# A four-layer graph network on one core: half of layer 2's softmax division moved from VectorE to GpSimd

## What is computed

```python
attn = jnp.einsum('bhnd,bhmd->bhnm', q, k) * scale
attn = jnp.where(attn_mask[None, None] == 0, -jnp.inf, attn)
attn = jax.nn.softmax(attn, axis=-1)
o = jnp.einsum('bhnm,bhmd->bhnd', attn, v).transpose(0, 2, 1, 3).reshape(b, n, d)
...
x = _layernorm(x + _L2_gnn_ref(x, ...), axis=-1)
```

## Time and profile before

| what | value |
|---|---|
| median of 3 runs | 1381.44 us (1379.06 to 1381.63) |
| the profiled execution: its own time | 1379.5 us |
| its span, first to last instruction | 1377.7 us |
| TensorE busy | 1345.8 us (98%), 10460 matmuls |
| VectorE busy | 1113.5 us (81%) |
| ScalarE busy | 784.8 us (57%) |
| GpSimd busy | 135.1 us (10%) |
| mean granted TensorE clock | 0.994 |

### The profile page before, as it was taken

One profiled execution on the slowest core, in us unless ns is written; L12 is line 12 of the kernel. 1 busy time (PEld: TensorE's weight loads), 2 busy tenths in 40 slices (PEclk: granted clock), 3 DMA queues, 4 the chain that ended last, 5 costly groups with the idle time before them and its releaser, 6 DMA issues.

```text
span 1377.7 us, 27138 instructions
## 1 busy us (share of the span) xinstructions
PE 1345.8 (98%) x10460; PEld 1141.8 (83%) x10460; DVE 1113.5 (81%) x2441; ACT 784.8 (57%) x1444; POOL 135.1 (10%) x194
## 2 busy tenths in 40 slices
PE   8999999999999999999999999999999999999996
PEld 8888878888888888888888888888888888888785
DVE  6889878788888879788887888879888787869555
ACT  3455656556665665656556565665656456654544
POOL 4010111010010100001010000101001010101000
PEclk9999999999999999999999999999999999999998
DMA  5000010100000001010100000000000100100100
GB/s 178 9 17 24 1 25 31 24 30 15 8 30 23 30 15 38 0 23 30 23 30 15 23 15 23 30 23 31 12 11 30 23 32 1 39 9 1 46 0 31
DMA packets 54671, 34.54 MB, mean 25 GB/s; under 512 B 34912, under 2 KB 51552, under 8 KB 54624
## 3 DMA queue, kind: packets, MB, share of 16 engines
q1 hardware_dynamic: 52816, 29.43, 7.2%
q0 software_dynamic: 1248, 3.94, 0.9%
q10 hardware_dynamic: 560, 0.52, 0.1%
HBM read 12.92 MB, written 8.39 MB: 15 GB/s over the span
## 4 chain that ended last, share of the span: by engine, by line
PE 89%; DVE 7%; ACT 2%; issue 1%; DMA 0%; POOLq 0%; DVEq 0%; POOL 0%; ACTq 0%
PE banks L122 22%; PE banks L124 21%; PE banks L123 21%; PE banks L667 8%; PE banks L662 3%; PE banks L937 3%; PE banks L826 2%; PE banks L841 2%; PE banks L743 2%; PE banks L815 2%; ACT l_htok L1468 1%; PE banks L804 1%; PE banks L1036 1%; DVE l_r L2522 0%; PE banks L735 0%
## 5 line engine op out<-in xcount | busy, mean ns | idle before, releaser
L1604 ACT ACTIVATE l_r<-banks,bias_r 128x512 f32<-128x512 f32 x90 | 61.4, 682 | 177.4 <-PE banks L124 177.3
L264 POOL TENSOR_TENSOR l_rstd<-l_mv,eps 128x4 f32<-128x4 f32 x47 | 19.2, 409 | 908.6 <-DVE l_mv L258 908.6
L1468 ACT ACTIVATE l_rh_hi<-l_r 128x512 fp32r<-128x512 f32 x90 | 56.4, 627 | 62.1 <-DVE l_r L2511 61.9
L1621 ACT ACTIVATE banks<-banks,bias_h 128x512 f32<-128x512 f32 x96 | 63.4, 662 | 25.4 <-PE banks L124 25.0
L122 PE MATMUL banks<-l_rh_hi,u_hi 128*128 128x512 f32 x180 | 76.1, 423 | 0.1
L1615 ACT ACTIVATE banks<-banks,bias_z 128x512 f32<-128x512 f32 x96 | 63.5, 663 | 19.7 <-PE banks L124 19.7
L278 ACT ACTIVATE y<-l_sum,l_offset,l_rstd 128x256 f32<-128x256 f32 x124 | 69.1, 598 | 6.1 <-DVE l_offset L272 6.0
L124 PE MATMUL banks<-l_rh_lo,u_hi 128*128 128x512 f32 x180 | 71.1, 395 | 0.0
L123 PE MATMUL banks<-l_rh_hi,u_lo 128*128 128x512 f32 x180 | 70.7, 393 | 0.0
L667 PE MATMUL banks<-adj_t,y 128*128 128x128 f32 x544 | 68.1, 277 | 1.5 <-DVE l_otok L2460 1.5
L1537 ACT ACTIVATE l_qk<-banks 128x512 f32<-128x512 f32 x64 | 38.3, 598 | 54.1 <-PE banks L124 53.4
(11 more groups left out here) (308 smaller groups left out, 4418.2 us busy)
## 6 DMA issues: line engine op xcount, KB each, us to landing
x_tok<-in_x_dram SPq DMA_DIRECT2D x15, 512.0 KB, 3.5
l_res<-y SPq DMA_DIRECT2D x15, 512.0 KB, 2.9
out_dram<-l_res SPq DMA_DIRECT2D x15, 512.0 KB, 2.9
l_vpair<-l_vstage SPq DMA_DIRECT2D x32, 128.0 KB, 3.0
w_raw<-in_L_gnn_w_w_dram POOLq DMA_DIRECT2D x3, 512.0 KB, 7.5
qkv_raw<-in_L_gnn_w_qkv_dram POOLq DMA_DIRECT2D x1, 768.0 KB, 4.5
l_res<-in_x_dram SPq DMA_DIRECT2D x1, 512.0 KB, 5.4
u_raw<-in_L_gnn_u_w_dram POOLq DMA_DIRECT2D x2, 256.0 KB, 7.4
```

Source lines behind the costliest of these rows:

```text
L1468: return nc.scalar.activation(out, source, ACT.Copy)
L1604: nc.scalar.activation(own(u).r[:, m, :], rz(u)[:, m, :], ACT.Tanh, scale=0.5, bias=w.biases["r"][:, m:m + 1]).then_inc(s.r_ready.of(u), 1)
L1621: nc.scalar.activation(hv(u)[:, m, :], hv(u)[:, m, :], ACT.Tanh, bias=w.biases["h"][:, m:m + 1]).then_inc(s.hv_ready.of(u), 1)
```

## The change

The division of tiles 2 and 3 of each unit's `prob` goes to GpSimd as a new step `l2_divide(u)`, which waits once for `inv` and then issues both multiplications. VectorE keeps tiles 0 and 1 (`BY_VECTOR = 2`). TensorE's turns of tiles 2 and 3 wait on a new semaphore that GpSimd increments. The sums of the next unit wait for the semaphore of the unit before, since they overwrite `inv`. The step gets a place in GpSimd's list in the loop, in the fill and in the drain.

```diff
+BY_VECTOR = 2
...
+        self.l2_prob_divided = one("l2_prob_divided", TILES - BY_VECTOR)
...
+        @within
+        def l2_divide(u):
+
+            pool.wait_ge(*s.l2_inv.at(u, TILES + 2))
+            for t in range(BY_VECTOR, TILES):
+                nc.gpsimd.tensor_tensor(b.prob[:, t, :, :], b.prob[:, t, :, :],
+                                        b.inv[:, t, :].unsqueeze(2).to_broadcast([P, HEADS, NODES]),
+                                        ALU.mult).then_inc(s.l2_prob_divided.sem, 1)
+
         def body(i):
+            l2_divide(i + 1)
             l3_root(i - 1)
             l2_inner_root(i + 1)
             l2_outer_root(i + 1)
...
             l0_root(1)
             l1_root(1)
+            l2_divide(0)
             l2_inner_root(0)
             l2_outer_root(0)
             l0_root(2)
+            l2_divide(1)
             l2_inner_root(1)
...
             l3_root(11)
+            l2_divide(13)
             l2_inner_root(13)
             l2_outer_root(13)
             l1_root(14)
+            l2_divide(14)
             l3_root(12)
             l0_root(15)
             l2_inner_root(14)
             l2_outer_root(14)
             l1_root(15)
+            l2_divide(15)
             l3_root(13)
...
         def l2_turn_prob(u, t):
-            pe.wait_ge(*s.l2_prob_shared.at(u, t + 1))
+            if t < BY_VECTOR:
+                pe.wait_ge(*s.l2_prob_shared.at(u, t + 1))
+            else:
+                pe.wait_ge(*s.l2_prob_divided.at(u, t + 1 - BY_VECTOR))
...
         def l2_sum(u, t):
             dve.wait_ge(*s.l2_exp.at(u, t + 1))
+            if t == 0:
+                past(dve, s.l2_prob_divided, u - 1, TILES - BY_VECTOR)
...
             l2_normal(i + 1, 0)
             l2_normal(i + 1, 1)
-            l2_normal(i + 1, 2)
-            l2_normal(i + 1, 3)
             l3_reset(i, 0, 1)
```

More of the change, by code:

```diff
@@ L396, in __init__ @@
         self.l2_exp, self.l2_prob_turned, self.l2_prob_t = one("l2_exp", TILES), one("l2_prob_turned", TILES), one("l2_prob_t", TILES)
-        self.l2_pv_done, self.l2_inv, self.l2_prob_shared = one("l2_pv_done", TILES), one("l2_inv", TILES + 2), one("l2_prob_shared", TILES)
+        self.l2_pv_done, self.l2_inv, self.l2_prob_shared = one("l2_pv_done", TILES), one("l2_inv", TILES + 2), one("l2_prob_shared", BY_VECTOR)
+        self.l2_prob_divided = one("l2_prob_divided", TILES - BY_VECTOR)
         self.l2_o_hi, self.l2_o_lo = one("l2_o_hi", CH), one("l2_o_lo", CH)
@@ L2797, in fill @@
             l0_leaky(2)
-            l2_normal(0, 2)
             l0_masked(2)
@@ L2801, in fill @@
             l0_max(2)
-            l2_normal(0, 3)
             l0_shift(2)
@@ L2852, in fill @@
             l3_reset(0, 0, 0)
-            for n in range(2, 4):
-                l2_normal(1, n)
             l3_reset(0, 0, 1)
@@ L2967, in drain @@
             l3_reset(12, 0, 0)
-            for n in range(1, 4):
-                l2_normal(13, n)
+            l2_normal(13, 1)
             l3_reset(12, 0, 1)
@@ L3073, in drain @@
             l0_offset(15)
-            for n in range(4):
+            for n in range(2):
                 l2_normal(14, n)
@@ L3148, in drain @@
             l3_low_rh(13, 2, 1)
-            for n in range(1, 4):
-                l2_normal(15, n)
+            l2_normal(15, 1)
             l3_difference(13, 2, 0)
```

## The result

| | before | with the change |
|---|---|---|
| median | 1379.86 us (5 runs, 1379.06 to 1381.63) | 1402.8 us (5 runs, 1402.11 to 1404.43) |
| ratio | | 1.0163, 95% interval 1.0152 to 1.0174 |
| span of the profiled execution | 1377.7 us | 1400.8 us |

The account below looks back on a forecast made before the run. TensorE, 98% busy, bounds the kernel, so what counts is when its inputs come. Loop 10.0, units 1, 14, 13, 15, 0 4.3 + 4.8 + 1.4 + 1.4 + 0.6, clock 2.6: +25.1 on 1379.5, said 1405; range 1388 to 1416.

Parts of the forecast that it names:

- the clock: TensorE's clock at half after the idle gaps in units 1 and 14: 1.3 us each, 2.6 in all.
- The loop: Units 2 to 12: TensorE loads tile 3 at +3.45 us instead of +2.54, +0.91 per unit, 10.0 for 11.
- the price of a division on GpSimd: One 128 x 512 multiplication on GpSimd, unhindered: 1.2 us, between 1.05 and 1.48.
- my lower end: Price of a GpSimd division if its two reads take turns: 1.05 us, for a total of 1397.
- Hindrance: VectorE and GpSimd instructions with two SBUF inputs hold each other, one at a time, in order of asking.
- the one-sided rival: VectorE is never held, GpSimd waits for each of its instructions: +0.45 us per loop unit, +17, 1396; 15%.
- The rule of the Trainium skill: VectorE instruction with two SBUF inputs and GpSimd instruction reading SBUF share a read interface; the second "fully blocks".
- The relief: Two of four divisions leave VectorE, 1.2 us per unit, running into its 0.90 us idle before l3_offset: worth nothing.
- Unit 1: Fill: GpSimd's division stands behind layer 0's root, and tile 2 meets an l3_low_rh; tile 3 late, +4.3 us.
- Unit 14: Drain: VectorE's offset waits for layer 0's root behind GpSimd's two divisions and layer 3's root; +4.8 us.
- Units 13, 15, 0: 13 and 15: GpSimd's tiles come between VectorE's divisions, +1.4 us each; 0: GpSimd still at a root, +0.6.

Follow-up runs that it names:

- e4: Kernel before, plus unused GpSimd work in each loop pass: a 128 x 4 addition and a memset of 128 x 512; 1380.22 us, ratio 1.0001.
- e3: Kernel before, plus unused GpSimd work in each loop pass: a 128 x 4 addition and a two-input 128 x 512 multiplication; 1389.13 us, ratio 1.0069.
- e7: As e6, with unit 0's division ahead of layer 1's root for unit 1 in GpSimd's list; 1375.99 us, ratio 0.9965 to the kernel before.
- e1_order: Changed kernel with GpSimd's list mended: unit 1's division ahead of a root, two roots ahead of unit 14's division; 1394.35 us, ratio to before 1.0095.
- e2: Changed kernel with the list of e1_order, GpSimd dividing tile 3 alone and VectorE tiles 0, 1 and 2; 1390.15 us, ratio 1.0074.
- e5: Kernel before, plus unused GpSimd work in each loop pass: a 128 x 4 addition and a 128 x 512 copy; 1386.70 us, ratio 1.0046.
- e6: List of e1_order, but GpSimd divides tile 0 alone, beside VectorE's row sums, and VectorE tiles 1 to 3; 1377.77 us, ratio to before 0.9983.

## Why the prediction was right

1405 us were forecast, 1402.8 measured; the forecast's sum was +25.1 us, and the two spans differ by 23.1. The mechanism of the forecast is the one that the runs show; the terms of the loop and of unit 1 were mis-sized, and the clock's other stretches were missing. By shifts of TensorE's matmuls between the two traces:

- **The loop.** Forecast +0.91 us for each of 11 units, 10.0 in all; measured 0.62, 6.8 in all. The order of events is as drawn: division, GpSimd's tile, division, GpSimd's tile, and VectorE's second division ends 2.14 us after its first began (forecast 2.35), GpSimd's second tile 3.04 us after (forecast 3.41). The step that was off is **the price of a division on GpSimd**. I took 1.2 us, and it is 1.04 (unit 14: two in 2.04), my lower end. With 1.05 the forecast had 6.7 us for the loop. That the write adds nothing to the two reads fits this price, and in e4 a memset ran beside VectorE's divisions without holding them.
- **Hindrance.** Forecast as mutual and in order of asking; e3 shows VectorE held by 0.84 us for one multiplication of GpSimd. The time alone would not have told this from the one-sided rival: 0.62 us a unit lies between that rival's 0.45 and the forecast's 0.91. VectorE's divisions recorded with 2.14 us and e3 do. The rule of the Trainium skill that was weighed ("SBUF — State Buffer", section "Who interferes with whom") holds here from both sides, also in what it exempts: memsets of GpSimd and row sums of VectorE are not in the way (e4: divisions at 2.50 us; e7: sum at 0.68, GpSimd's division at 1.04).
- **The relief.** It was costed at nothing, with VectorE's wait for the root as its cover. Nothing was right, the cover was not needed: VectorE had no time freed. In unit 3 its divisions and the reset end 3.59 us after the first began (291.96 to 295.55), against 3.09 in the earlier trace rows, and it waits for the root for 0.90 us as before.
- **Unit 1.** Forecast +4.3 us and 1.3 for the clock; tile 3 came 3.4 us late, the slow clock behind it cost 1.6. The difference is again the price of a division, and that GpSimd's tile 2 did not meet the `l3_low_rh` that I let it meet: that one came only at 124.45, held up 4.05 us by ScalarE's copy.
- **Unit 14.** Forecast +4.8 and 1.3; measured 4.4 and 1.4. e1_order confirms both places: mended, unit 1 costs 1.3 us in place of 5.0, and unit 14 0.5 in place of 5.8, the slow clock included.
- **Units 13, 15, 0.** Forecast 1.4, 1.4, 0.6; measured 1.0, 1.7, 0.6.
- **Missing.** The clock stood at half for 6.8 us at the start in place of 3.4 (+1.5 us), and once at the entry of the loop (+2.2 us with the longer wait there); in the tail a slow stretch of the kernel before did not come (-1.6). The sum of all is 23.0 us, against 23.1 of the spans. That these three belong to the change is not shown. At the start e1_order has 77.7 us up to unit 0 like the changed kernel, e2 75.9, and no division of GpSimd's stands before that; at the entry of the loop other traces with nearly the same wait have no slow stretch; and in the tail e3 and e5 lack it too.

So the closeness of 1405 to 1402.8 is partly luck: 3.2 us too much in the loop and 0.9 in unit 1 stand against 2.1 us net that the clock did elsewhere.

## What to carry to other kernels

Moving elementwise work with two SBUF inputs from VectorE to GpSimd gave nothing here while VectorE itself ran such instructions: the two took turns, and GpSimd's turn was the longer one (0.84 us against VectorE's 0.60). Put GpSimd's piece beside VectorE instructions that read one SBUF input, even if that needs a small step drawn ahead. For a reduction e7 shows it. For a VectorE instruction with its other operand in PSUM only small additions show it: in the kernel before, GpSimd's 128 x 4 addition takes 0.20 us beside `late_lo<-banks,late_hi` (12 times), and 0.55 us beside `l_rh_lo<-l_r,l_rh_hi`, both of whose inputs are in SBUF. And when an engine with a written list gets a long step, walk its list for every place: here two of six places cost 5.0 and 5.8 us (3.0 of it the slow clock behind them), together more than the eleven loop units (6.8).

## What was not expected of the hardware

Work whose result nobody uses slows the kernel by 9 us, 0.7% (e3), and GpSimd's price to VectorE goes by the streams that it reads: 0.41 us for one and 0.84 for two, per 512 columns. The record of an instruction includes its standing still: VectorE's second division of unit 3 and the reset behind it are recorded with 1.53 us each where 0.68 is usual, so a mean of busy time over a group (1442 ns for GpSimd's division) says neither what it costs nor what it would cost alone (1.04 us). The clock's slow stretches near the start, the loop's entry and the tail differ between executions. Near the start they last 0 us in the trace of e7, 3.4 in that of the kernel before and 6.8 in that of e6, and by 60 us, where no division has run yet, TensorE's matmuls lie 0.5 us earlier in e7 and 1.4 us later in e6 than in the kernel before. The 11 runs of e6 reach from 1374.42 us at a mean granted clock of 0.996 to 1381.23 at 0.990.
